# Loading and splitting the shared experts' weights of a decoder layer: no staging ring, gate weights split inside the last two cross-attention steps

## What is computed

```python
x = x + attn(layernorm(x))
x = x + xattn(layernorm(x), ctx)              # softmax((q Wq)(k Wk)^T / 8) (v Wv) Wo, 16 heads
x = x + ffn(layernorm(x))
# ffn:
shared_out = (silu(x @ shared_gate_w) * (x @ shared_up_w)) @ shared_down_w   # 512->1024->512
logits = x @ gate_w; topk = argmax(logits); xs = x * sigmoid(max(logits))
routed_out = expert[topk](xs)                 # 32 experts, same shape
return shared_out + routed_out
```

## Time and profile before

| | |
|---|---|
| median of 3 runs | 2887.55 us (2887.39 to 2888.48) |
| profiled execution | 2887.28 us, span 2885.6 us, mean granted clock of TensorE 0.991 |
| busy in the span | PE 96%, weight loads 79%, DVE 62%, ACT 55%, POOL 35% |
| self-attention and start | about 0 to 800 us |
| cross-attention, with its tail | to about 1456 us |
| shared experts | 1467 to about 2010 us |
| routed experts | from there to the end |

### The profile page before, as it was taken

The page is one execution under the profiler, slowest core; times in us unless marked ns, Lnnn a source line. Parts: engine busy times, 40 slices in busy tenths (PEclk is TensorE's granted clock), DMA queues, the critical chain, the costliest instruction groups (busy, mean ns, idle before and its releaser), DMA issues.

```text
span 2885.6 us, 46298 instructions
## 1 busy us (share of the span) xinstructions
PE 2781.1 (96%) x13288; PEld 2290.8 (79%) x13289; DVE 1802.6 (62%) x2744; ACT 1593.0 (55%) x2743; POOL 1015.5 (35%) x692
## 2 busy tenths in 40 slices
PE   7999999999889999999889999999999999999998
PEld 6888888888777887888767888887788888888886
DVE  6566666667776655567553434435885954776776
ACT  6888888887665455555431111111564743565665
POOL 5888888887522121222200000000232322332332
PEclk9999999999999999999999999999999999999999
DMA  1000000002121101110231111112986964786884
GB/s 63 26 26 11 25 25 29 25 11 81 62 66 45 44 29 53 44 33 28 65 117 59 58 58 58 58 58 72 346 304 226 366 218 132 281 293 220 292 284 179
DMA packets 190791, 322.70 MB, mean 112 GB/s; under 512 B 23528, under 2 KB 49128, under 8 KB 190720
## 3 DMA queue, kind: packets, MB, share of 16 engines
q1 hardware_dynamic: 179440, 296.61, 29.9%
q0 software_dynamic: 11280, 25.20, 2.6%
HBM read 286.86 MB, written 46.66 MB: 116 GB/s over the span
## 4 chain that ended last, share of the span: by engine, by line
PE 82%; DVE 8%; ACT 4%; issue 3%; DMA 1%; POOL 1%; DVEq 0%; ACTq 0%; SPq 0%; POOLq 0%
PE d_pG L1981 8%; PE d_pU L1981 8%; PE a_pS L47 4%; PE a_pS L49 4%; PE a_pS L48 4%; PE a_pO L47 4%; PE a_pO L49 4%; PE a_pO L48 4%; PE d_pD L49 3%; PE d_pD L47 3%; PE d_pD L48 3%; PE c_pD L47 2%; PE c_pD L49 2%; PE c_pD L48 2%; PE c_pG L47 2%
## 5 line engine op out<-in xcount | busy, mean ns | idle before, releaser
L157 POOL TENSOR_TENSOR a_pL<-a_p,a_pH 128x1024 fp32r<-128x1024 f32 x256 | 617.8, 2419 | 166.2 <-DVE a_p L348 164.3
L1237 DVE TENSOR_TENSOR e_wL<-e_raw,e_wH 128x1024 fp32r<-128x1024 f32 x384 | 450.2, 1216 | 36.2 <-PE d_pU L1981 21.5
L348 DVE TENSOR_TENSOR a_p<-a_r,a_pS 128x1024 f32<-128x1024 f32 x256 | 312.2, 1220 | 244.0 <-ACT a_r L165 236.9
L1232 ACT CAST e_wH<-e_raw 128x1024 fp32r<-128x1024 f32 x384 | 384.4, 1052 | 85.4 <-PE d_pD L49 59.2
L705 POOL TENSOR_TENSOR b_S<-b_S,b_ri 128x512 f32<-128x512 f32 x128 | 133.4, 1042 | 500.6 <-DVE b_ri L862 500.6
L165 ACT ACTIVATE a_r<-a_pS 128x1024 f32<-128x1024 f32 x256 | 261.8, 1023 | 81.0 <-PE a_pS L49 78.6
L165 ACT ACTIVATE a_pH<-a_r 128x1024 fp32r<-128x1024 f32 x256 | 271.9, 1062 | 9.1
L722 ACT ACTIVATE b_S<-b_S,b_nm 128x128 f32<-128x128 f32 x512 | 198.8, 392 | 39.5 <-DVE b_nm L857 39.0
L1473 POOL DMA_INDIRECT out<-d_og,c_iw x46 | 86.6, 1882 | 358.9 <-DVE d_og L1855 358.9
L47 PE MATMUL a_pS<-a_qH,a_kH 128*128 (+1 forms) x512 | 205.8, 402 | 1.2 <-DVE a_p L348 1.2
L47 PE MATMUL a_pO<-a_pH,a_vH 128*128 128x512 f32 x512 | 199.8, 390 | 1.5 <-POOL a_pL L157 1.5
(11 more groups left out here) (307 smaller groups left out, 7263.7 us busy)
## 6 DMA issues: line engine op xcount, KB each, us to landing
e_raw<-in_L_ffn_routed_gate_w SPq DMA_DIRECT2D x256, 256.0 KB, 4.5
e_raw<-in_L_ffn_routed_up_w SPq DMA_DIRECT2D x256, 256.0 KB, 5.7
e_raw<-in_L_ffn_routed_down_w SPq DMA_DIRECT2D x128, 512.0 KB, 6.7
a_xb<-in_x SPq DMA_DIRECT2D x8, 1024.0 KB, 5.4
x<-a_base SPq DMA_DIRECT2D x32, 256.0 KB, 2.3
b_xr<-x SPq DMA_DIRECT2D x32, 256.0 KB, 3.3
x<-b_xr SPq DMA_DIRECT2D x32, 256.0 KB, 3.1
c_xb<-x SPq DMA_DIRECT2D x32, 256.0 KB, 2.9
```

The lines of the kernel that those rows point to most:

```text
L157: nc.gpsimd.tensor_tensor(pL[:, j % RING, :, :], p[:, j % 2, :, :], pH[:, j % RING, :, :].bitcast(F32), ALU.subtract).then_inc(s["low"], 1)
L348: v.tensor_tensor(p[:, j % 2, :, :], r[:, j % 2, :, :], pS[j % 2][:, :, :], ALU.mult).then_inc(s["p"], 1)
L1232: copy(self.wH[n][:, :, :], self.raw[n][:, :, :]).then_inc(self.s["high"], 1)
L1237: unit.tensor_tensor(self.wL[n][:, :, :], self.raw[n][:, :, :], self.wH[n][:, :, :].bitcast(self.F32), self.sub).then_inc(self.s["low"], 1)
```

## The change

The staging ring and `split_weights` go. Each piece is loaded straight into a place of its own. The gate and the down weights are loaded where their low parts will stand (`raw_g` over `wgL`, `raw_d` over `wdL`), and the subtraction works in place. The up weights have 16 KB of their own (`raw_u`). SP loads a piece once the high part of the piece four before it is made.

The four gate pieces are loaded when the last query product is done (`q_ps`). Their high parts are made on ACT at the end of steps 62 and 63, two pieces in each, and their low parts on DVE at the end of its list for the same steps, ahead of the next step's work. The up pieces are split in the tail. The down pieces are loaded when the last `project` is done, and split at hidden steps 2 to 5 of group 0. PE waits for the down pieces one by one. A sigmoid of one element on ACT in the tail loads the sigmoid table there.

```diff
-def split_weights(nc, ctx, tag, parts, mybir, stage=None):
...
@@ cross_attention, scalar body
+                if j >= NPAIR - 2 and last:
+                    aside(j - NPAIR + 2)
@@ cross_attention, vector body
-                if j == 1 and last:
-                    aside()
+                if j in (1, 6, 7) and last:
+                    aside(j)
@@ feed_forward, places
-    stage = c.at(168 * KB, "stage", [P, 3, 2 * C], F32)
-    xb = c.at(180 * KB, "xb", [P, 2, C], F32)
+    raw_g, raw_d = c.at(16 * KB, "raw_g", [P, KC, IC * P], F32), c.at(128 * KB, "raw_d", [P, IC, C], F32)
+    raw_u = c.at(168 * KB, "raw_u", [P, KC, IC * P], F32)
+    xb = c.at(188 * KB, "xb", [P, 2, C], F32)
@@ feed_forward, sync
+        def load_weights(n):
+            wait(sp, s["w_high"], n + 1 - KC)
+            sp.dma_start(piece(n, raw_g, raw_u, raw_d), piece(n, wg_v, wu_v, wd_v)).then_inc(s[f"w_in{n % KC}"], 16)
+
         def ending(reload, store, free):
+            sp.wait_ge(b["q_ps"], QUERIES)
+            for n in range(KC):
+                load_weights(n)
             sp.wait_ge(b["score"], QUERIES)
             load(0, 0)
             load(1, 1)
             sp.dma_start(rw[:, :, :], gate_w.rearrange("(a p) n -> p a n", p=P)).then_inc(s["g_in"], 16)
-            load_parts(sp, 0, 3)
             reload(GROUPS - 1, 0)
             reload(GROUPS - 1, 1)
+            for n in range(KC, 2 * KC):
+                load_weights(n)
             for i in range(2, GT):
                 sp.wait_ge(s["normed"], i - 1)
                 load(i, i)
-            load_parts(sp, 3, 6)
             store(TILES - 4, 0)
             reload(GROUPS - 1, 2)
-            load_parts(sp, 6, 2 * KC)
             store(TILES - 3, 1)
             reload(GROUPS - 1, 3)
+            sp.wait_ge(b["wo"], TILES)
+            for n in range(2 * KC, 3 * KC):
+                load_weights(n)
             store(TILES - 2, 2)
             store(TILES - 1, 3)
...
-        load_parts(sp, 2 * KC)
@@ feed_forward, scalar
+        def w_high(n):
+            act.wait_ge(s[f"w_in{n % KC}"], 16 * (n // KC + 1))
+            nc.scalar.activation(piece(n, wgH, wuH, wdH), piece(n, raw_g, raw_u, raw_d), ACT.Copy).then_inc(s["w_high"], 1)
+
+        def aside(i):
+            w_high(2 * i)
+            w_high(2 * i + 1)
+        cross["scalar"](act, aside)
         act.wait_ge(s["g_in"], 16)
         nc.scalar.activation(rH, rw[:, :, :], ACT.Copy).then_inc(s["rH"], 1)
-        high_parts(act, 2, KC)
+        nc.scalar.activation(first_silu[:, :], ident[0:1, 0:1], ACT.Sigmoid).then_inc(s["warm"], 1)
+        w_high(KC)
         x_high(0, 0)
-        high_parts(act, KC, KC + 2)
-        x_high(1, 1)
-        x_high(2, 2)
-        high_parts(act, KC + 2, 2 * KC)
-        x_high(3, 3)
+        for n in range(KC + 1, 2 * KC):
+            w_high(n)
+        for i in range(1, GT):
+            x_high(i, i)
...
-                if first:
-                    high_parts(act, 2 * KC + i // 2, 2 * KC + (i + 1) // 2)
+                if first and 2 <= i < 2 + KC:
+                    w_high(2 * KC + i - 2)
@@ feed_forward, vector
+        def w_low(n):
+            dve.wait_ge(s["w_high"], n + 1)
+            sub(piece(n, wgL, wuL, wdL), piece(n, raw_g, raw_u, raw_d), piece(n, wgH, wuH, wdH)).then_inc(s["w_low"], 1)
+
+        def aside(j):
+            if j == 1:
+...
+            else:
+                w_low(2 * (j - 6))
+                w_low(2 * (j - 6) + 1)
@@ feed_forward, vector ending
             add(g, 0)
             norm(0, 2)
-            low_parts(dve, 0, 1)
             add(g, 1)
+            x_low(0, 0)
             norm(0, 3)
-            low_parts(dve, 1, 2)
-            x_low(0, 0)
             out_stats(g, 0)
-            low_parts(dve, 2, 3)
+            w_low(4)
             out_stats(g, 1)
-            low_parts(dve, 3, 4)
+            w_low(5)
             x_low(1, 1)
             x_low(2, 2)
             add(g, 2)
-            low_parts(dve, 4, 5)
             out_stats(g, 2)
...
-            low_parts(dve, 5, 7)
+            w_low(6)
             x_low(3, 3)
             add(g, 3)
-            low_parts(dve, 7, 8)
+            w_low(7)
             out_stats(g, 3)
@@ feed_forward, tensor
-                pe.wait_ge(low_done, KC)
+                pe.wait_ge(s["w_low"], KC)
...
-                if first and i == 0:
-                    pe.wait_ge(low_done, len(parts))
...
                     if i == 0:
                         pe.wait_ge(s["hL"], IC * g + c + 1)
+                        if first:
+                            pe.wait_ge(s["w_low"], 2 * KC + c // 2 + 1)
```

More of the change, by code:

```diff
@@ L706, in gpsimd, with scalar @@
         groups(pool, body)
-    def scalar(act):
+    def scalar(act, aside):
         def x_high(t, i):
@@ L1331, in feed_forward @@
          ("const g_in rH rL x_in0 x_in1 r_in0 r_in1 normed xt xH xL gate up sig gated h hH hL logit_ps lt logit top own score xs xs_out"
-          " down sum out0 out1").split()}
+          " down sum out0 out1 w_in0 w_in1 w_in2 w_in3 w_high w_low warm").split()}
     rs = {n: ctx.enter_context(nc.semaphore("r_" + n)) for n in
@@ L1341, in feed_forward, with piece @@
     KNOWN = TILES - 2 * GT
[L1342 to L1348, removed]
+    wg_v, wu_v, wd_v = (w.rearrange("(a p) n -> p a n", p=P) for w in (Wg, Wu, Wd))
+    def piece(n, gate, up, down):
+        a = n % KC
+        return (gate[:, a, :], up[:, a, :], down[:, 2 * a:2 * a + 2, :])[n // KC]
     HALF = weights.half
@@ L1525, in x_high @@
             nc.scalar.activation(xH[:, :, i * P:(i + 1) * P], source, ACT.Copy).then_inc(s["xH"], 1)
-        cross["scalar"](act)
-        act.wait_ge(b["q_ps"], QUERIES)
-        high_parts(act, 0, 2)
+        def w_high(n):
[5 more added lines that the diff above has]
+        cross["scalar"](act, aside)
         act.wait_ge(s["g_in"], 16)
         nc.scalar.activation(rH, rw[:, :, :], ACT.Copy).then_inc(s["rH"], 1)
-        high_parts(act, 2, KC)
+        nc.scalar.activation(first_silu[:, :], ident[0:1, 0:1], ACT.Sigmoid).then_inc(s["warm"], 1)
+        w_high(KC)
         x_high(0, 0)
-        high_parts(act, KC, KC + 2)
-        x_high(1, 1)
-        x_high(2, 2)
-        high_parts(act, KC + 2, 2 * KC)
-        x_high(3, 3)
+        for n in range(KC + 1, 2 * KC):
+            w_high(n)
+        for i in range(1, GT):
+            x_high(i, i)
         def shared(g, first, last):
@@ L1705, in indices @@
             v.tensor_copy(index[:, :], idx_f[:, :]).then_inc(rs["index"], 1)
[L1707 to L1711, removed]
+        def w_low(n):
[3 more added lines that the diff above has]
+            if j == 1:
+                dve.wait_ge(b["seen"], KNOWN)
+                link = Link(dve, s["own"])
+                layernorm_stats(nc, link, stats, 1, mv, var, tmp, rstd, mybir, 0, KNOWN)
+                assert link.n == SL
+            else:
+                w_low(2 * (j - 6))
+                w_low(2 * (j - 6) + 1)
         def ending(t_low, a_low, add, out_stats):
@@ L1771, in shared @@
                 sub(hL[:, i, :], h[:, i % 2, :], hH[:, i, :]).then_inc(s["hL"], 1)
-                if first:
-                    low_parts(dve, 2 * KC + i // 2, 2 * KC + (i + 1) // 2)
+                if first and 2 <= i < 2 + KC:
+                    w_low(2 * KC + i - 2)
                 if i == IC - 3 and not last:
@@ L1936, in shared @@
                 if first and i == 0:
-                    pe.wait_ge(low_done, 2 * KC)
+                    pe.wait_ge(s["w_low"], 2 * KC)
                 if i == 1:
```

## The result

The changed kernel takes 2879.7 us (median of 8 runs, 2877.47 to 2880.19), the one before 2887.11 in the same comparison (8 runs). The ratio is 0.9973, 95% interval 0.9962 to 0.9983: 7.4 us faster. The forecast was 2876.3, so the direction and the range of 8 in 10 (2872.0 to 2880.9) hold, the narrower own range (2874.5 to 2878) doesn't, and the size was 11.2 us where 7.4 came. The profiled execution of the changed kernel took 2879.42 us, 7.86 less than that of before, and its span is 2877.7.

What follows compares the result with a forecast made beforehand. PE, busy 96% of the span, was taken as the bound, with gains only where it idles or runs at low clock. 2887.28 - 3.8 - 7.4 = 2876.1, plus 0.27 for the median: 2876.3 us; 8-in-10 range 2872.0 to 2880.9.

Steps and rivals of the forecast that it cites:

- The cost on DVE: Steps 62 and 63: DVE waits for high parts, then subtracts, delaying `t_low` and PE; 7.5 us, ends 7.5 to 8.6.
- PE's list is 7.5 us late: From `values(62)` on, PE runs late by 7.4 us plus 0.1 for a slower first matmul after a gap.
- the low clock behind the longer gap: After the 7.4 us gap, low clock on `values(61)` and some `project` matmuls ends before PE's next wait; priced at nothing.
- low clock in the rows from 1436 on: PE's rows from about `values(62)` on: a low clock there would show the forecast wrong.
- The rule: Long idle gaps send PE to the low clock; one low stretch more, 2.3 us, makes 2878.6.
- rival 1: Tail: clock falls once or twice more, 2.3 us per low stretch; 2878.6 or 2880.9; chance 0.13.
- The new start of the gate product: Tail: gate product starts at 1465.05 after 1.3 us idle, full clock; up product starts 3.8 us earlier.
- Rival 3: Tail: store and reload delay `add(g, 2)` and so the gate product; 2880.4, or 2882.7 with low clock; chance 0.06.
- a first gate matmul 1.5 us earlier than before: Tail, sign of being right: the gate product's first matmul starts 1.5 us earlier than before.
- The down product: Group 0: no wait for down pieces, 5.9 us between transposes; gain 7.4 us (4.2 gap, 3.1 clock).
- The table load: ACT in the tail: the sigmoid table load moves to about 1448, where ACT waits; priced at nothing, 1.3 us if uncovered.
- the loads: Gate pieces loaded from about 1408.0: pieces 0 and 1 land long before ACT comes to them.

Runs made afterwards that it cites:

- old_places: Changed kernel with the down pieces split at hidden steps 1, 3, 5, 7 as before, PE still waiting piece by piece; 2876.90 us.
- old_places_wait_all: Changed kernel with the down part undone: pieces split at hidden steps 1, 3, 5, 7, PE waiting for all before the first down product; 2883.88 us.
- one_step_later: Changed kernel with gate pieces 0 and 1 subtracted at the end of step 63, piece 2 in the tail, piece 3 after the last `t_low`; 2868.07 us.
- down_only: Kernel before with only the down pieces loaded in place, split at hidden steps 2 to 5 and awaited one by one; 2880.49 us.
- low_in_tail: Changed kernel with DVE's four gate subtractions moved from steps 62 and 63 into the tail, ACT's copies staying; 2868.29 us.
- after_again: Changed kernel run once more with no edit; 2879.81 us.
- wait_all: Changed kernel, down pieces split at hidden steps 2 to 5, PE waiting for all of them before the first down product; 2878.73 us.
- no_warm: Changed kernel without the early sigmoid on ACT; 2877.98 us.

## Why the prediction was right in direction and too large in size

**The cost on DVE: right in mechanism, mis-sized.** The stall, the order of what waits behind it and the second stall came as written. The term "PE's list is 7.5 us late" measured 51.7 - 41.4 = 10.3. That is 2.8 us too little, and it is the whole of the miss up to the down phase: from `values(60)` to the transposes of the next group's second tile, before 1528.30 - 1414.12 = 114.2, after 1519.71 - 1413.88 = 105.8, so 8.4 gained where 11.2 was forecast.

The failed step is the sentence that let the low clock behind the longer gap cost nothing. It looked only at the 18 matmuls of `project` and missed two other things that run at it or after it. First, the transposes of step 62 ran wholly at the low clock, 1.88 us against 1.21 before. ACT's `t_high(62)`, the exponentials and so the second stall hang on them: 0.7. Second, `values(62)` started at the low clock again after the second gap: six matmuls at 0.43 with a first of 0.80 are 1.5 us more than at the full clock. The rest, 0.6, is `values(60)` at the low clock; old_places, without it, has 51.1. Together 2.8. The terms are read from the rows. No run changed the clock by itself. The prediction had named low clock in the rows from 1436 on as a sign of being wrong, and `values(62)` at 1437.70 is that sign.

**The rule and rival 1.** The low level came behind the 6.83 us gap (0.52 in its stretch) and again behind the second wait, of 2.92 us. Rival 1, with 0.13, is what happened, by one mechanism more than it named: it priced a low stretch after the waits at 2.3 us. The trace agrees with the Trainium skill, *TensorE: Matmul & The Clock Gate*, "Why this matters for your kernels", which asks for no long idle gaps between bursts; by it the sum was 2878.6, and the profiled execution took 2879.42. The nearness of the number is partly luck: the rival's 2.3 us were to be one low stretch, and 1.4 came at `values(62)`, 0.7 at the transposes, 0.6 at `values(60)`, and 1.1 in the routed experts ("After it"). I had weighed one favourable profile against it.

**The new start of the gate product: right from the transposes on.** From the last transposes 1.41 us idle (1.3 forecast), full clock (1.00 in its stretch), the up product 4.9 us after the transposes (4.8). `add(g, 2)` had its reload in time, piece 7 as well. Rival 3 didn't come. The sign that the prediction named for this part, a first gate matmul 1.5 us earlier than before, did not come: it stands at 1467.60, 0.9 us later than 1466.67, because PE's list was later than forecast.

**The down product: right**, 5.91 us, and two runs show that either of its two edits is enough. Of the 7.4, 3.1 are low clock, and in old_places_wait_all the same gap cost 1.9 of it.

**The table load and the loads: right at nothing.**

**After it.** Of 8.6 us at the transposes of group 0, 7.9 are left at the end of the span. In all twelve profiles the time behind those transposes is the same within 0.5 us but for one block, the first of the routed experts. PE waits 2.9 to 3.4 us for `d_h` there, and the block behind the wait runs at the full level, at the low one, or partly at each. Changed, before and old_places:

```profile
2045.90 1.11 PE L1976 MATMUL d_pT<-ident,d_h 128*128 128x128 f32 x4 [3.24 <-DVE d_h L1820]
...
2053.64 0.60 PE L1976 MATMUL d_pT<-ident,d_h 128*128 128x128 f32 x4
```

```profile
2054.52 0.66 PE L1992 MATMUL d_pT<-ident,d_h 128*128 128x128 f32 x4 [3.14 <-DVE d_h L1836]
...
2061.19 0.60 PE L1992 MATMUL d_pT<-ident,d_h 128*128 128x128 f32 x4
```

```profile
2047.14 0.66 PE L1976 MATMUL d_pT<-ident,d_h 128*128 128x128 f32 x4 [3.29 <-DVE d_h L1820]
...
2052.22 0.60 PE L1976 MATMUL d_pT<-ident,d_h 128*128 128x128 f32 x4
```

From transposes to transposes these are 7.7, 6.7 and 5.1 us. So the changed kernel lost 1.1 us there against before. The block takes 5.1 us in old_places and one_step_later, 6.5 to 6.7 in before, down_only and old_places_wait_all, and 7.7 in the other seven. No edit touches it. What decides it is open. The block alone differs by up to 2.7 us, as much as several medians in the table do.

**What was left on the table.** The first half by itself has a median 3.3 us under before (old_places_wait_all), of which its profile puts 0.9 at the up product. Without the stall the changed kernel gains 11.4 us more: low_in_tail and one_step_later are 18.9 and 19.3 us faster than before. The change closed a gap of 10.5 us and made PE's list 10.3 us late in the same chain. At the up product 1.0 us was left as a gain in the profiles, where 3.8 were forecast: from `values(60)` to it are 1471.70 - 1414.12 = 57.6 us before and 1470.49 - 1413.88 = 56.6 after.

## What to carry to other kernels

In an engine with one list, an instruction placed aside delays everything queued behind it by its wait and its work, and each consumer pays what its slack doesn't cover. Before placing one, ask when its input is made, and who is already waiting for what stands behind it. One pair of subtractions at the end of step 63 was free here, within the 2.4 us of slack of `values(62)`. The two pairs placed right behind their copies cost 11 us: PE was already waiting behind the first pair and paid its wait and its work in full, and the second pair's work came on top of a wait that had used up the slack. Where a forecast rests on a hidden low-clock stretch, follow every short producer in it too, not only the longest block of matmuls.

## What the runs showed of the hardware that was not expected

- A table load on ACT costs its 1.28 us and nothing beside: the copy ahead of it ended at 1450.58, the sigmoid behind it started at 1451.89.
- The same gap gives the low clock in one profile and not in another. The gap of 2.45 us ahead of `values(60)` ended at the low level in five profiles (changed, after_again, old_places_wait_all, wait_all, no_warm) and at the full one in the seven others, with the same instructions on PE up to there. The gap of about 3.3 us ahead of the first routed transposes was followed by a block of 5.1, 6.5 to 6.7 or 7.7 us. After the same 4.24 us ahead of the down product, the block took 13.3 us before and 12.0 in old_places_wait_all. The changed kernel, profiled twice, showed the same levels both times, so whether this differs from execution to execution or from kernel to kernel is open.
